# Maxima over the last 260 keys, taken off VectorE in layers 2 and 3 of a four-layer gated cross-attention model

## The chip, the cores and the metric

The kernel runs on one core of one Trainium2 chip. The metric is the device time of one execution in microseconds (us), the median of several runs. The core has TensorE (PE; its weight loads are shown as PEld), VectorE (DVE), ScalarE (ACT), GpSimd (POOL) and SyncE, which issues DMAs (SP).

## The reference

Four layers, each a cross-attention from 1024 queries to 6404 context keys of width 128, followed by a feed-forward part, both gated and added to x. The change touches the attentions of layers 2 and 3, which have 16 heads of width 8. Cut to what matters:

```python
q = heads(norm(x) @ Wq + bq)           # 1024 x 16 x 8
k = heads(ctx @ Wk + bk)               # 6404 x 16 x 8
v = heads(ctx @ Wv + bv)
w = softmax(q @ k.T / sqrt(8))         # over 6404 keys; layer 2 masks keys too
x = x + tanh(g) * ((w @ v) @ Wo + bo)
```

A softmax in this form subtracts the largest score of each query before the exponential.

## The kernel before

`narrow_attention` computes one such layer. It cuts the work into 32 units, one for each head and half of the queries (512 columns, `CH`), so there are 64 units in the two layers. Each unit needs two passes over the keys.

**Maxima.** TensorE computes scores with 128 queries down the partitions and keys along the row, into two slots of two PSUM banks each (banks 4 to 7). A step is two matmuls of 512 keys (`max_score`, L1692) and one VectorE reduction over the 1024 scores (L1858). The 6404 keys are six pairs of 512 and a rest of 260 (`REM`). For each of four groups of 128 queries there are six wide steps, and two more steps reduce the rest of two groups each (L1861), 26 steps in all. VectorE then reduces the seven partial maxima to a negated maximum (`nm`, L1867) and splits it into two bfloat16 parts (`nmp`, L1868 and L1869).

**Exponentials.** `turn_nm` (L1704) transposes the split maximum on TensorE, and ScalarE copies it into the top rows of Q (L1791), so that the next scores come with the maximum already subtracted. TensorE then computes the scores again with 128 keys down the partitions (`score`, L1680), 51 tiles a unit, the last of four keys. ScalarE takes the exponential of each (L1800). The scores and the transposed maxima share a ring of three PSUM banks, 0 to 2: the taker with number n is written when ScalarE has read number n - 3. After each four tiles the weighted sums of the batch before (`weigh`, L1716) run in four column groups into bank 3, and ScalarE copies that bank out once a unit (L1784).

**Order.** All loops are written out by hand, and each engine takes its work in order. TensorE puts the maximum matmuls of the coming units between the scores of the present one: it is a whole unit and 14 matmuls ahead (`ahead = MM + 2 * LEAD`), and behind score t it issues those from `ahead + MM * u + t * MM // ST` on. A step's first matmul waits until VectorE has reduced the step two before it. The transposition for unit u+1 stands behind tile 42 of unit u (`NM_AT` is 43). In the last unit of each layer no maxima are left, and a filler matmul of the same shape (`keep_warm`, L1722) takes their place; that unit also holds the sums over the denominators and the projections. SyncE loads K and Q for each unit ahead of time. GpSimd does nothing in this phase.

The end of one pass on TensorE, with the function that decides when a bank may be written:

```python
for t in range(ST):
    score(u, t)
    ...
    for m in range(ahead + MM * u + t * MM // ST, ahead + MM * u + (t + 1) * MM // ST):
        if m < MM * UNITS:
            max_score(m)
    if t == NM_AT - 1 and u + 1 < UNITS:
        turn_nm(u + 1)
```

Of the kernel before, what the change touches and what calls it, by code (L numbers as in the profile page):

```python
# [9 lines left out]
ALU = mybir.AluOpType  # L10
ACT = mybir.ActivationFunctionType
AX = mybir.AxisListType

P = 128
# [3 lines left out]
S = 6404  # L18
ST = -(-S // P)
LAST = S - (ST - 1) * P  # L20
CH = 512
HALVES = N // CH
# [35 lines left out]
class Core:  # L58
# [18 lines left out]
    def sb(self, name, shape, dtype, held=None):  # L77
        return (held or self.held).enter_context(self.nc.sbuf_tensor(name, shape, dtype))
# [1234 lines left out]
def narrow_attention(c, name, w, gate, masked, scratch):  # L1313
    nc = c.nc
# [3 lines left out]
    ROWS = TOP + 7 * DH  # L1318
    VW = DH + 1
    UNITS = HEADS * HALVES  # L1320
    UQ = CH // P
    PAIR = 2 * CH
    FULL = S // PAIR
    REM = S - FULL * PAIR
    STEPS = UQ * FULL + UQ // 2
    MM = 2 * STEPS
    LEAD = 7
    NM_AT = 43
    SPREAD_AT, PROJECT_AT = (20, 24), (40, 50)
    BATCH = 4  # L1330
    BATCHES = -(-ST // BATCH)
    MROW = 64
# [3 lines left out]
    with ExitStack() as held:  # L1336
        sb = lambda n, s, d=FP32: c.sb(f"{name}_{n}", s, d, held)
# [2 lines left out]
        K = [sb(f"K{i}", [P, S], BF16) for i in range(2)]  # L1340
        Q = [sb(f"Q{i}", [P, CH], BF16) for i in range(3)]
        V = sb("V", [P, ST, HEADS, VW])
        mx = sb("mx", [P, 2, UQ, FULL + 1])
        nm = sb("nm", [P, 2, UQ])
        nmp = sb("nmp", [P, 2, UQ, 2], BF16)
        acc = sb("acc", [P, 2, CH])
# [242 lines left out]
        def step_no(u, i):  # L1589
            return STEPS * u + i  # L1590

        def ring_no(u, t):
            return 1 + (ST + 1) * u + t + (1 if t >= NM_AT and u + 1 < UNITS else 0)

        def nm_no(u):
            return 0 if u == 0 else 1 + (ST + 1) * (u - 1) + NM_AT

        def step_at(i):
            if i < UQ * FULL:
                return [(i // FULL, (i % FULL) * PAIR + half * CH, CH) for half in range(2)]  # L1600
            return [(2 * (i - UQ * FULL) + half, FULL * PAIR, REM) for half in range(2)]

        def slot(step):
            return 4 + 2 * (step % 2)

        ACC = 3
        with phase(nc, "chain", "scored", "exped", "weighed", "max_scored", "maxed", "nm_ready", "acc_out", "acc_clear",
                   "max_in_0", "max_in_1", "max_in_2", "exp_in_0", "exp_in_1", "exp_in_2", "out_in_0", "out_in_1",
                   "den_out", "normal", "projected", "last_projected", "summed") as (
                block, chain, scored, exped, weighed, max_scored, maxed, nm_ready, acc_out, acc_clear,  # L1610
                max_in_0, max_in_1, max_in_2, exp_in_0, exp_in_1, exp_in_2, out_in_0, out_in_1, den_out, normal,
                projected, last_projected, summed):
            out_in = (out_in_0, out_in_1)
            OUT_MOVES = 2 * BATCH
# [6 lines left out]
            def loads_by(u):  # L1621
                return sum(6 if v % HALVES == 0 else 3 for v in range(u % 3, u + 1, 3))
# [49 lines left out]
            def _(pe):  # L1672
# [10 lines left out]
                def max_score(m):  # L1683
# [11 lines left out]
                    if half == 1:  # L1695
                        last.then_inc(max_scored, 1)

                def turn_nm(u):
                    n = nm_no(u)
                    pe.wait_ge(nm_ready, u + 1)  # L1700
                    if n >= 3:
                        pe.wait_ge(exped, n - 2)
                    for j in range(UQ):
                        last = nc.tensor.matmul(c.banks(n % 3)[0:2, j * P:(j + 1) * P], nmp[:, u % 2, j, :], c.identb[:],  # L1704
                                                start=True, stop=True)
                    last.then_inc(scored, 1)
# [38 lines left out]
                    last.then_inc(last_projected, 1)  # L1745

                ahead = MM + 2 * LEAD
                for m in range(ahead):
                    max_score(m)
                    if m == MM + 7:  # L1750
                        turn_nm(0)
                for u in range(UNITS):
                    if u == UNITS - 1:
                        pe.wait_ge(maxed, STEPS * UNITS)
                    for t in range(ST):
                        score(u, t)
                        if u == UNITS - 1:
                            keep_warm(u)
                        for m in range(ahead + MM * u + t * MM // ST, ahead + MM * u + (t + 1) * MM // ST):
                            if m < MM * UNITS:  # L1760
                                max_score(m)
                        if t == NM_AT - 1 and u + 1 < UNITS:
# [15 lines left out]
            @block.scalar  # L1778
            def _(act):
                def take_acc(u):  # L1780
                    act.wait_ge(weighed, BATCHES * (u + 1))
                    if u >= 2:
                        act.wait_ge(out_in[u % 2], 16 * OUT_MOVES * (u // 2))
                    nc.scalar.copy(acc[:, u % 2, :], c.banks(ACC)).then_inc(acc_out, 1)  # L1784

                def take_nm(u):
                    n = nm_no(u)
                    act.wait_ge(scored, n + 1)
                    if u >= 3:
                        act.wait_ge(scored, ring_no(u - 3, ST - 1) + 1)  # L1790
                    nc.scalar.copy(Q[u % 3][0:2, :], c.banks(n % 3)[0:2, :]).then_inc(exped, 1)  # L1791

                take_nm(0)
                for u in range(UNITS):
                    for t in range(ST):
                        n, r, batch = ring_no(u, t), rows_of(t), BATCHES * u + t // BATCH
                        act.wait_ge(scored, n + 1)
                        if t % BATCH == 0 and batch >= 2:
                            act.wait_ge(weighed, batch - 1)
                        nc.scalar.activation(prob[0:r, batch % 2, t % BATCH, :], c.banks(n % 3)[0:r, :], ACT.Exp,  # L1800
                                             scale=SCALE).then_inc(exped, 1)
                        if t == NM_AT - 1 and u + 1 < UNITS:
# [3 lines left out]
                take_acc(UNITS - 1)  # L1806

            @block.vector
            def _(dve):
# [42 lines left out]
                for u in range(UNITS):  # L1852
                    for i in range(STEPS):
                        step = step_no(u, i)
                        j, a, k = step_at(i)[0]
                        dve.wait_ge(max_scored, step + 1)
                        if i < UQ * FULL:
                            nc.vector.tensor_reduce(mx[:, u % 2, j, i % FULL:i % FULL + 1], c.banks(slot(step), 2),  # L1858
                                                    AX.X, ALU.max).then_inc(maxed, 1)
                        else:  # L1860
                            nc.vector.tensor_reduce(mx[:, u % 2, j:j + 2, FULL],  # L1861
                                                    c.ps[:, slot(step):slot(step) + 2, 0:REM],
                                                    AX.X, ALU.max).then_inc(maxed, 1)
                    dve.wait_ge(maxed, step_no(u, STEPS - 1) + 1)
                    if u >= 2:
                        dve.wait_ge(scored, nm_no(u - 2) + 1)
                    link(nc.vector.tensor_reduce(nm[:, u % 2, :], mx[:, u % 2, :, :], AX.X, ALU.max, negate=True))  # L1867
                    link(nc.vector.tensor_copy(nmp[:, u % 2, :, 0], nm[:, u % 2, :]))  # L1868
                    nc.vector.tensor_tensor(nmp[:, u % 2, :, 1], nm[:, u % 2, :], nmp[:, u % 2, :, 0], ALU.subtract  # L1869
                                            ).then_inc(nm_ready, 1)  # L1870
                for f in range(HALVES):
                    add_groups(f)
# [533 lines left out]
```

## Time and profile before

| | |
|---|---|
| median of 3 runs | 5270.39 us (5267.61 to 5272.48) |
| span of the profiled execution, the time given of it | 5269.8 us |
| PE busy | 4827.1 us, 92% |
| DVE busy | 4327.4 us, 82% |
| ACT busy | 3096.7 us, 59% |
| POOL busy | 1940.9 us, 37% |
| one unit in layers 2 and 3 | 31.62 us |

Busy shares are of the whole span; layers 2 and 3 take about the last 40% of it and have no GpSimd work in their main phase. A group of instructions is listed with its line, engine, operation, output and input; then its busy time and the mean duration of one in ns, then the idle time of the engine just before it and what ended that. Durations of matmuls overlap, so that a pitch is read from starts.

### The profile page before, as it was taken

What the parts mean: (1) busy time and instruction counts of PE and PEld (TensorE: products, weight loads), DVE (VectorE), ACT (ScalarE), POOL (GpSimd) and SP (SyncE); (2) the same over time, 40 slices, a digit from 0 to 9 for tenths busy, and PEclk for the clock granted to TensorE, in tenths of its full rate; (3) what the DMA queues carried; (4) which work ended last, traced back from release to release, by engine and by line L of the source; (5) the groups of instructions that cost most, each with busy time, mean ns of one, the idle gap of its engine ahead of it and who ended that gap; (6) DMA issues with size and microseconds to landing.
All of it is one profiled execution on the core that took longest, in us unless ns stands there. A gap on an engine that the chain in (4) does not pass through costs nothing. (4 is left out here: it accounts for less than half of the span.)

```text
span 5269.8 us, 74714 instructions
## 1 busy us (share of the span) xinstructions
PE 4827.1 (92%) x26357; PEld 1891.5 (36%) x26366; DVE 4327.4 (82%) x4358; ACT 3096.7 (59%) x6111; POOL 1940.9 (37%) x1522
## 2 busy tenths in 40 slices
PE   8938999999999999999995699999998699999997
PEld 5623454544545454544442222222222322222222
DVE  7648878788787878878886699999996599999996
ACT  3313454454545454444442288888886288888886
POOL 0014878787787878787783100000000100000000
PEclk9968999999999999999997699999998699999998
DMA  1024334242333334142210211111110211111110
GB/s 36 5 89 117 95 92 112 60 124 51 103 81 98 98 82 122 40 123 64 51 38 15 78 29 29 29 34 29 29 23 2 78 28 29 28 29 33 30 23 6
DMA packets 171375, 298.10 MB, mean 57 GB/s; under 512 B 39061, under 2 KB 108577, under 8 KB 167393
## 3 DMA queue, kind: packets, MB, share of 16 engines
q1 hardware_dynamic: 169420, 292.95, 21.8%
q8 instruction: 213, 3.49, 0.3%
q14 instruction: 158, 1.29, 0.1%
q10 hardware_dynamic: 1584, 0.37, 0.0%
HBM read 187.39 MB, written 101.25 MB: 55 GB/s over the span
## 5 line engine op out<-in xcount | busy, mean ns | idle before, releaser
L1858 DVE TENSOR_REDUCE a_mx<-ps 128x1 f32<-128x1024 f32 x1536 | 1814.5, 1220 | 71.0 <-PE ps L1692 54.5
L1800 ACT ACTIVATE a_prob<-ps 128x512 f32<-128x512 f32 (+1 forms) x3264 | 1699.7, 601 | 288.1 <-PE ps L1680 283.3
L1227 POOL TENSOR_TENSOR tot_p<-tot_p,prob 128x512 f32<-128x512 f32 (+1 forms) x922 | 1300.4, 1410 | 401.5 <-ACT prob L1103 315.3
L1103 ACT ACTIVATE prob<-ps 128x512 f32<-128x512 f32 (+1 forms) x1512 | 801.1, 608 | 866.1 <-PE ps L979 865.2
L1151 DVE TENSOR_REDUCE mx<-ps 128x1 f32<-128x1024 f32 x896 | 1047.3, 1214 | 222.4 <-PE ps L956 222.4
L1692 PE MATMUL ps<-a_K,a_Q 59*128 59x512 bf16 (+1 forms) x3328 | 1094.7, 386 | 56.4 <-DMA a_Q<-q_stack_dram 44.5
L1680 PE MATMUL ps<-a_Q,a_K 59*128 59x512 bf16 (+1 forms) x3264 | 988.7, 383 | 55.8 <-ACT a_prob L1800 49.5
L1716 PE MATMUL ps<-a_prob,a_V 128*9 128x512 f32 x6528 | 871.8, 596 | 10.9 <-ACT a_acc L1784 10.9
L978 PE MATMUL ps<-QA,KA 128*128 128x512 f32 (+1 forms) x1888 | 841.7, 446 | 0.0
L990 PE MATMUL ps<-prob,V 128*64 128x512 f32 x3024 | 801.1, 599 | 0.7 <-ACT prob L1103 0.7
L979 PE MATMUL ps<-QB,KB 128*128 128x512 f32 (+1 forms) x1888 | 746.1, 395 | 0.0
L1173 DVE TENSOR_TENSOR tot_d<-tot_d,prob 128x512 f32<-128x512 f32 x539 | 629.3, 1167 | 134.6 <-ACT prob L1103 114.8
L1680 PEld LDWEIGHTS ps<-a_Q,a_K 59*128 59x128 bf16 (+1 forms) x3264 | 240.6, 93 | 1114.5 <-ACT a_prob L1800 920.3
L978 PEld LDWEIGHTS ps<-QA,KA 128*128 128x128 f32 (+1 forms) x1888 | 351.4, 186 | 279.0 <-ACT prob L1103 109.7
L2299 POOL MEMSET f_ones<- 128x128 f32 x1 | 0.2, 210 | 1097.5 <-POOLq L43 1097.5
L2208 POOL MEMSET f_spread<- 8x512 f32 x1 | 0.5, 515 | 1095.4 <-SPq L41 1095.4
L956 PE MATMUL ps<-KM,QM 64*128 64x512 bf16 (+1 forms) x1920 | 319.1, 383 | 69.2 <-DVE mx L1151 42.6
L979 PEld LDWEIGHTS ps<-QB,KB 128*128 128x128 f32 (+1 forms) x1888 | 354.0, 187 | 61.8 <-issue 26.8
L1692 PEld LDWEIGHTS ps<-a_K,a_Q 59*128 59x128 bf16 x3328 | 240.3, 94 | 357.5 <-DVE a_mx L1858 301.8
L990 PEld LDWEIGHTS ps<-prob,V 128*64 128x64 f32 x3024 | 224.3, 136 | 392.5 <-issue 323.6
L1227 POOL TENSOR_TENSOR tot_p<-tot_p,h 128x512 f32<-128x512 f32 x230 | 323.6, 1407 | 99.8 <-ACT h L1103 78.0
L1103 ACT ACTIVATE h<-ps 128x512 f32<-128x512 f32 (+1 forms) x376 | 212.5, 607 | 220.4 <-PE ps L979 220.3
(415 smaller groups left out, 3772.8 us busy)
## 6 DMA issues: line engine op xcount, KB each, us to landing
a_K<-k_stack_dram SPq DMA_DIRECT2D x128, 300.2 KB
k_hi_dram<-hi_s SPq DMA_DIRECT2D x112, 256.0 KB, 2.2
k_lo_dram<-lo_s SPq DMA_DIRECT2D x112, 256.0 KB, 2.4
KA<-k_hi_dram SPq DMA_DIRECT2D x64, 384.0 KB, 4.3
KA<-k_lo_dram SPq DMA_DIRECT2D x64, 384.0 KB, 5.6
KB<-k_hi_dram SPq DMA_DIRECT2D x64, 384.0 KB, 6.6
k_bf_dram<-bf_s SPq DMA_DIRECT2D x112, 128.0 KB, 1.8
KM<-k_bf_dram SPq DMA_DIRECT2D x32, 448.0 KB
```

The lines of the kernel that those rows point to most:

```text
L978: nc.tensor.matmul(out, KA[:, cols], QA[u % 2][:], start=True, stop=False)
L979: nc.tensor.matmul(out, KB[:, cols], QB[u % 2][:], start=False, stop=True).then_inc(scored, 1)
L990: last = nc.tensor.matmul(c.banks(ACC)[DH * g:DH * (g + 1), :], V[:, t, DH * side:DH * (side + 1)], prob_of(u, t), start=(t < 2), stop=(t ...
L1103: nc.scalar.activation(prob_of(u, t)[0:r, :], c.banks(n % 3)[0:r, :], ACT.Exp, scale=SCALE).then_inc(exped, 1)
L1151: nc.vector.tensor_reduce(mx[:, u % 2, j, i % FULL:i % FULL + 1], c.banks(slot(n), 2), AX.X, ALU.max).then_inc(released, 1)
L1173: nc.vector.tensor_tensor(tot_d[0:r, u % 2, :], tot_d[0:r, u % 2, :], p, ALU.add).then_inc(totalled_d, 1)
L1227: nc.gpsimd.tensor_tensor(tot_p[0:r, u % 2, :], tot_p[0:r, u % 2, :], p, ALU.add).then_inc(totalled_p, 1)
L1680: nc.tensor.matmul(c.banks(n % 3)[0:r, :], K[(u // HALVES) % 2][0:ROWS, t * P:t * P + r], Q[u % 3][0:ROWS, :], start=True, stop=True).then ...
L1692: last = nc.tensor.matmul(c.banks(slot(step) + half)[:, 0:k], Q[u % 3][MROW:MROW + ROWS, j * P:(j + 1) * P], K[(u // HALVES) % 2][MROW:MRO ...
L1716: last = nc.tensor.matmul(c.banks(ACC)[32 * g:32 * g + VW, :], V[:, t, u // HALVES, :], prob[:, (BATCHES * u + b) % 2, g, :], start=(t < B ...
L1800: nc.scalar.activation(prob[0:r, batch % 2, t % BATCH, :], c.banks(n % 3)[0:r, :], ACT.Exp, scale=SCALE).then_inc(exped, 1)
L1858: nc.vector.tensor_reduce(mx[:, u % 2, j, i % FULL:i % FULL + 1], c.banks(slot(step), 2), AX.X, ALU.max).then_inc(maxed, 1)
```

## The change

The steps over the last 260 keys leave the maxima's slots and VectorE. Four times in a unit (behind tiles 6, 13, 20 and 27, and at the start for unit 0) TensorE computes 260 scores of one group of 128 queries into a bank of the exponentials' ring, and ScalarE copies them to SBUF (`tail`). GpSimd folds them in five rounds, each time taking the maximum of the two halves as max(a - b, 0) + b, from 260 to 130, 65, 33, 17 and 9 columns for each of four groups; the nine go into `mx` beside the six others. VectorE waits for the fold before it takes the negated maximum, over 15 values instead of 7. The split into two bfloat16 parts moves to GpSimd, and the transposition waits for that.

```diff
-    STEPS = UQ * FULL + UQ // 2
+    STEPS = UQ * FULL
+    TAIL_AT = (6, 13, 20, 27)
+    LEFT = 9
...
+                def score_tail(u, j):
+                    n = tail_no(u, j)
+                    if j == 0:
+                        pe.wait_ge(max_in[u % 3], 16 * loads_by(u))
+                    if n >= 3:
+                        pe.wait_ge(exped, n - 2)
+                    nc.tensor.matmul(c.banks(n % 3)[:, 0:REM], Q[u % 3][MROW:MROW + ROWS, j * P:(j + 1) * P],
+                                     K[(u // HALVES) % 2][MROW:MROW + ROWS, FULL * PAIR:S], start=True, stop=True
+                                     ).then_inc(scored, 1)
...
                 def turn_nm(u):
                     n = nm_no(u)
-                    pe.wait_ge(nm_ready, u + 1)
+                    pe.wait_ge(nm_cut, 2 * (u + 1))
...
+                        if t in TAIL_AT and u + 1 < UNITS:
+                            score_tail(u + 1, TAIL_AT.index(t))
...
+                def take_tail(u, j):
+                    n = tail_no(u, j)
+                    act.wait_ge(scored, n + 1)
+                    if j == 0 and u >= 1:
+                        act.wait_ge(folded, u)
+                    nc.scalar.copy(tail[:, j, :], c.banks(n % 3)[:, 0:REM]).then_inc(exped, 1)
...
+                def fold_tail(u):
+                    pool.wait_ge(exped, tail_no(u, UQ - 1) + 1)
+                    if u >= 2:
+                        pool.wait_ge(nm_ready, u - 1)
+                    src, w = tail, REM
+                    for dst in (half, fold, half, fold, None):
+                        n = -(-w // 2)
+                        to = mx[:, u % 2, :, FULL:FULL + LEFT] if dst is None else dst[:, :, 0:n]
+                        a, b, d = src[:, :, 0:n], src[:, :, w - n:w], over[:, :, 0:n]
+                        link(nc.gpsimd.tensor_tensor(d, a, b, ALU.subtract))
+                        link(nc.gpsimd.tensor_scalar(d, d, 0.0, None, ALU.max))
+                        last = nc.gpsimd.tensor_tensor(to, d, b, ALU.add)
+                        if dst is None:
+                            last.then_inc(folded, 1)
+                        else:
+                            link(last)
+                        src, w = dst, n
+
+                def cut_nm(u):
+                    pool.wait_ge(nm_ready, u + 1)
+                    if u >= 2:
+                        pool.wait_ge(scored, nm_no(u - 2) + 1)
+                    nc.gpsimd.tensor_copy(nmp[:, u % 2, :, 0], nm[:, u % 2, :]).then_inc(nm_cut, 1)
+                    pool.wait_ge(nm_cut, 2 * u + 1)
+                    nc.gpsimd.tensor_tensor(nmp[:, u % 2, :, 1], nm[:, u % 2, :], nmp[:, u % 2, :, 0], ALU.subtract
+                                            ).then_inc(nm_cut, 1)
...
-                        else:
-                            nc.vector.tensor_reduce(mx[:, u % 2, j:j + 2, FULL],
-                                                    c.ps[:, slot(step):slot(step) + 2, 0:REM],
-                                                    AX.X, ALU.max).then_inc(maxed, 1)
...
                     dve.wait_ge(maxed, step_no(u, STEPS - 1) + 1)
+                    dve.wait_ge(folded, u + 1)
                     if u >= 2:
-                        dve.wait_ge(scored, nm_no(u - 2) + 1)
-                    link(nc.vector.tensor_reduce(nm[:, u % 2, :], mx[:, u % 2, :, :], AX.X, ALU.max, negate=True))
-                    link(nc.vector.tensor_copy(nmp[:, u % 2, :, 0], nm[:, u % 2, :]))
-                    nc.vector.tensor_tensor(nmp[:, u % 2, :, 1], nm[:, u % 2, :], nmp[:, u % 2, :, 0], ALU.subtract
+                        dve.wait_ge(nm_cut, 2 * (u - 1))
+                    nc.vector.tensor_reduce(nm[:, u % 2, :], mx[:, u % 2, :, :], AX.X, ALU.max, negate=True
                                             ).then_inc(nm_ready, 1)
```

## Rows read from the trace of the kernel before

**Rows 1.** The page's first line.

```profile
span 5269.8 us, 74714 instructions
```

**Rows 2.** Groups by line; busy us, mean ns, idle before it and its releasers.

```profile
L1858 DVE TENSOR_REDUCE a_mx<-ps 128x1 f32<-128x1024 f32 x1536 | 1814.5, 1220 | 71.0 <-PE ps L1692 54.5
```

**Rows 3.** VectorE's timeline in a steady unit; start, length, instructions merged.

```profile
3300.07 3.76 DVE L1858 TENSOR_REDUCE a_mx<-ps 128x1 f32<-128x1024 f32 x3
...
3331.69 3.71 DVE L1858 TENSOR_REDUCE a_mx<-ps 128x1 f32<-128x1024 f32 x3
```

**Rows 4.** VectorE's timeline at the start of the phase in layer 2.

```profile
2985.35 28.22 DVE L1858 TENSOR_REDUCE a_mx<-ps 128x1 f32<-128x1024 f32 x24 [9.03 <-PE ps L1692]
...
3015.51 4.70 DVE L1858 TENSOR_REDUCE a_mx<-ps 128x1 f32<-128x1024 f32 x4
```

**Rows 5.** TensorE's timeline over one batch of four tiles in that unit.

```profile
3315.54 0.39 PE L1680 MATMUL ps<-a_Q,a_K 59*128 59x512 bf16 x1
...
3316.62 0.39 PE L1680 MATMUL ps<-a_Q,a_K 59*128 59x512 bf16 x1
...
3316.94 1.05 PE L1716 MATMUL ps<-a_prob,a_V 128*9 128x512 f32 x8
3317.92 0.39 PE L1680 MATMUL ps<-a_Q,a_K 59*128 59x512 bf16 x1
```

**Rows 6.** ScalarE's timeline around and in the last unit of layer 3.

```profile
5193.51 1.54 ACT L1800 ACTIVATE a_prob<-ps 128x512 f32<-128x512 f32 x3 [0.31 <-PE ps L1680]
5195.32 2.06 ACT L1800 ACTIVATE a_prob<-ps 128x512 f32<-128x512 f32 x4 [0.27 <-PE ps L1680]
...
5202.68 2.06 ACT L1800 ACTIVATE a_prob<-ps 128x512 f32<-128x512 f32 x4 [0.31 <-PE ps L1680]
5205.05 2.06 ACT L1800 ACTIVATE a_prob<-ps 128x512 f32<-128x512 f32 x4 [0.31 <-PE ps L1680]
```

**Rows 7.** ScalarE's timeline in the steady unit: its end, and the maximum's batch.

```profile
3306.24 1.54 ACT L1800 ACTIVATE a_prob<-ps 128x512 f32<-128x512 f32 x3 [0.31 <-PE ps L1680]
3308.60 2.07 ACT L1800 ACTIVATE a_prob<-ps 128x512 f32<-128x512 f32 x4 [0.81 <-PE ps L1680]
...
3332.58 1.57 ACT L1800 ACTIVATE a_prob<-ps 128x512 f32<-128x512 f32 x3 [0.31 <-PE ps L1680]
...
3335.44 2.07 ACT L1800 ACTIVATE a_prob<-ps 128x512 f32<-128x512 f32 x4 [0.36 <-PE ps L1680]
```

**Rows 8.** Groups by line and shape, GpSimd's and one of ScalarE's.

```profile
L1227 POOL TENSOR_TENSOR tot_p<-tot_p,prob 128x512 f32<-128x512 f32 x897 | 1268.9, 1415 | 357.5 <-ACT prob L1103 271.5 <-ACT h L1103 0.4
L1245 POOL TENSOR_TENSOR y<-y,fin_s 128x512 f32<-128x512 f32 x32 | 50.9, 1591 | 2.5
L1232 POOL TENSOR_TENSOR tot_p<-tot_p,tot_d 128x512 f32<-128x512 f32 x32 | 40.6, 1268 | 4.6
L1224 POOL COPY tot_p<-prob 128x512 f32<-128x512 f32 x26 | 15.8, 609 | 55.4 <-ACT prob L1103 55.4
L1530 POOL TENSOR_SCALAR a_keepm<-a_keepv 128x51 f32<-128x51 f32 x1 | 0.3, 255 | 0.2 <-POOL a_keepv L1529 0.2
L1529 POOL COPY a_keepv<-keep 4x1 f32<-4x1 f32 x1 | 0.2, 178 | 0.1
...
L1054 ACT CAST hi_s<-ps 128x260 fp32r<-128x260 f32 x8 | 3.1, 393 | 0.0
```

**Rows 9.** Stretches of 1 us in the last unit; busy us (instructions) of each engine, granted clock, DMA.

```profile
5210.00:5211.00 1.00, 0.50 (x6) 0.10 (x2) 0.95 (x2) 0.84 (x2) 0.00 (x0) 1.00 0.00 0
...
5214.00:5215.00 1.00, 1.00 (x8) 0.00 (x0) 0.97 (x2) 0.56 (x2) 0.00 (x0) 0.50 0.00 0
...
5217.00:5218.00 1.00, 1.00 (x10) 0.11 (x4) 0.97 (x2) 0.85 (x2) 0.00 (x0) 1.00 0.00 0
```

**Rows 10.** TensorE's timeline there.

```profile
5213.32 1.90 PE L1716 MATMUL ps<-a_prob,a_V 128*9 128x512 f32 x8
...
5216.88 1.04 PE L1716 MATMUL ps<-a_prob,a_V 128*9 128x512 f32 x8
```

More of the change, by code:

```diff
@@ L1342, in narrow_attention @@
         V = sb("V", [P, ST, HEADS, VW])
-        mx = sb("mx", [P, 2, UQ, FULL + 1])
+        mx = sb("mx", [P, 2, UQ, FULL + LEFT])
+        tail = sb("tail", [P, UQ, REM])
+        half, fold, over = sb("half", [P, UQ, REM // 2]), sb("fold", [P, UQ, REM // 4]), sb("over", [P, UQ, REM // 2])
         nm = sb("nm", [P, 2, UQ])
@@ L1590, in step_no, with takes_ring, tail_no @@
             return STEPS * u + i
+        ring = {}
+        def takes_ring(kind, u, i):
+            ring[kind, u, i] = len(ring)
+        for j in range(UQ):
+            takes_ring("tail", 0, j)
+        takes_ring("nm", 0, 0)
+        for u in range(UNITS):
+            for t in range(ST):
+                takes_ring("score", u, t)
+                if t in TAIL_AT and u + 1 < UNITS:
+                    takes_ring("tail", u + 1, TAIL_AT.index(t))
+                if t == NM_AT - 1 and u + 1 < UNITS:
+                    takes_ring("nm", u + 1, 0)
         def ring_no(u, t):
-            return 1 + (ST + 1) * u + t + (1 if t >= NM_AT and u + 1 < UNITS else 0)
+            return ring["score", u, t]
         def nm_no(u):
-            return 0 if u == 0 else 1 + (ST + 1) * (u - 1) + NM_AT
+            return ring["nm", u, 0]
+        def tail_no(u, j):
+            return ring["tail", u, j]
         def step_at(i):
-            if i < UQ * FULL:
-                return [(i // FULL, (i % FULL) * PAIR + half * CH, CH) for half in range(2)]
-            return [(2 * (i - UQ * FULL) + half, FULL * PAIR, REM) for half in range(2)]
+            return [(i // FULL, (i % FULL) * PAIR + half * CH, CH) for half in range(2)]
         def slot(step):
@@ L1607, in narrow_attention @@
         with phase(nc, "chain", "scored", "exped", "weighed", "max_scored", "maxed", "nm_ready", "acc_out", "acc_clear",
+                   "folding", "folded", "nm_cut",
                    "max_in_0", "max_in_1", "max_in_2", "exp_in_0", "exp_in_1", "exp_in_2", "out_in_0", "out_in_1",
@@ L1610, in narrow_attention @@
                 block, chain, scored, exped, weighed, max_scored, maxed, nm_ready, acc_out, acc_clear,
-                max_in_0, max_in_1, max_in_2, exp_in_0, exp_in_1, exp_in_2, out_in_0, out_in_1, den_out, normal,
+                folding, folded, nm_cut, max_in_0, max_in_1, max_in_2, exp_in_0, exp_in_1, exp_in_2, out_in_0, out_in_1, den_out, normal,
                 projected, last_projected, summed):
@@ L1747, in _ @@
                 ahead = MM + 2 * LEAD
+                for j in range(UQ):
+                    score_tail(0, j)
                 for m in range(ahead):
@@ L1761, in _ @@
                                 max_score(m)
+                        if t in TAIL_AT and u + 1 < UNITS:
+                            score_tail(u + 1, TAIL_AT.index(t))
                         if t == NM_AT - 1 and u + 1 < UNITS:
@@ L1791, in take_nm @@
                     nc.scalar.copy(Q[u % 3][0:2, :], c.banks(n % 3)[0:2, :]).then_inc(exped, 1)
+                def take_tail(u, j):
[4 more added lines that the diff above has]
+                    nc.scalar.copy(tail[:, j, :], c.banks(n % 3)[:, 0:REM]).then_inc(exped, 1)
+                for j in range(UQ):
+                    take_tail(0, j)
                 take_nm(0)
@@ L1801, in _ @@
                                              scale=SCALE).then_inc(exped, 1)
+                        if t in TAIL_AT and u + 1 < UNITS:
+                            take_tail(u + 1, TAIL_AT.index(t))
                         if t == NM_AT - 1 and u + 1 < UNITS:
@@ L1806, in _ @@
                 take_acc(UNITS - 1)
+            @block.gpsimd
+            def _(pool):
+                link = Chain(pool, folding)
+                def fold_tail(u):
[23 more added lines that the diff above has]
+                                            ).then_inc(nm_cut, 1)
+                fold_tail(0)
+                cut_nm(0)
+                for u in range(1, UNITS):
+                    fold_tail(u)
+                    cut_nm(u)
             @block.vector
@@ L1856, in _ @@
                         dve.wait_ge(max_scored, step + 1)
-                        if i < UQ * FULL:
-                            nc.vector.tensor_reduce(mx[:, u % 2, j, i % FULL:i % FULL + 1], c.banks(slot(step), 2),
-                                                    AX.X, ALU.max).then_inc(maxed, 1)
-                        else:
-                            nc.vector.tensor_reduce(mx[:, u % 2, j:j + 2, FULL],
-                                                    c.ps[:, slot(step):slot(step) + 2, 0:REM],
-                                                    AX.X, ALU.max).then_inc(maxed, 1)
+                        nc.vector.tensor_reduce(mx[:, u % 2, j, i % FULL:i % FULL + 1], c.banks(slot(step), 2),
+                                                AX.X, ALU.max).then_inc(maxed, 1)
                     dve.wait_ge(maxed, step_no(u, STEPS - 1) + 1)
+                    dve.wait_ge(folded, u + 1)
                     if u >= 2:
-                        dve.wait_ge(scored, nm_no(u - 2) + 1)
-                    link(nc.vector.tensor_reduce(nm[:, u % 2, :], mx[:, u % 2, :, :], AX.X, ALU.max, negate=True))
-                    link(nc.vector.tensor_copy(nmp[:, u % 2, :, 0], nm[:, u % 2, :]))
-                    nc.vector.tensor_tensor(nmp[:, u % 2, :, 1], nm[:, u % 2, :], nmp[:, u % 2, :, 0], ALU.subtract
+                        dve.wait_ge(nm_cut, 2 * (u - 1))
+                    nc.vector.tensor_reduce(nm[:, u % 2, :], mx[:, u % 2, :, :], AX.X, ALU.max, negate=True
                                             ).then_inc(nm_ready, 1)
```

## The prediction

> **What bounds the kernel now.** I read the page first, then the groups by line, then the timelines of one steady unit on VectorE, ScalarE and TensorE, then the same timeline in the last unit, where one of the engines has nothing to do. The span is 5269.8 us [rows 1], and nothing else is given of this execution's time; the median of the runs is 5270.39 us, 0.6 more, so I add differences to 5270. By the groups the maxima look like the bound: L1858 is the costliest group and VectorE sits idle before it for only 71 us in 1536 times [rows 2]. A steady unit of layers 2 and 3 takes 31.62 us (3300.07 to 3331.69, both the first maximum after a negated maximum) [rows 3]; there are 64 of them.
>
> But VectorE alone would be faster. At the start of the phase, with no exponentials, a whole unit of its work, 24 wide maxima, two narrow ones and three small operations, runs from 2985.35 to 3015.51, 30.16 us, 1.174 us for a wide maximum ((28.22 - 1.22) / 23) [rows 4]. What really sets the pace shows in one batch of four key tiles [rows 5]. First score at 3315.54, fourth score at 3316.62, when the first exponential has given back its bank of the ring of three; the weighted sums at 3316.94; the next first score at 3317.92. That is 2.38 us for a batch, and two wide maxima need 2.35. Is it VectorE that holds this loop? In the last unit no maxima are left, only fillers of the same shape, and the batch still takes 2.37 us (5202.68 to 5205.05) [rows 6]. So the loop is TensorE and ScalarE handing over three banks, and VectorE merely just keeps up. VectorE shows as the bound at one place: the three-tile batch at a unit's end takes 2.36 us (3306.24 to 3308.60) [rows 7], and 1.81 us (5193.51 to 5195.32) where there are no maxima to wait for [rows 6]. Without VectorE a unit is 31.62 - 0.55 = 31.07 us.
>
> **What is removed.** Two narrow maxima and two small operations leave VectorE, about 30.16 - 24 x 1.174 = 1.98 us less 0.2 for the remaining reduction, 1.8 us a unit. Because of the loop that is worth only the 0.55 us at the end of each unit; after the change just one maximum matmul falls there instead of two, and VectorE has slack. The last two units of each layer have no such wait, so 60 x 0.55 = -33 us. At each start 26 steps become 24, which is 1.5 us, against four copies ahead of everything and GpSimd's split: I take -1 us for both layers. The first fold lies under the first 28 us of maxima and costs nothing.
>
> **What is added to the ring.** Four times a unit (behind tiles 6, 13, 20, 27) a 260-column matmul takes a bank and ScalarE copies it. A ScalarE read of 128x260 took 393 ns [rows 8]; an exponential takes 0.60 us by itself and its pitch in a row of four is (2.06 - 0.60) / 3 = 0.49 us [rows 6], 0.52 with the handover of a bank. The loop is tight, so it matters which bank the last score of the batch waits for. Behind tiles 6 and 13 there is one more full exponential ahead of the weighted sums: +0.52 each. Behind tile 20 the fifth taker waits for the short copy: +0.30. Behind tile 27 the copy's own matmul is last and short: +0.41. Sum 1.75 us. The trace has this case already: the batch in which the negated maximum takes a bank is 2.86 us (3332.58 to 3335.44) [rows 7], +0.49. Bounds: 4 x 0.30 = 1.2 and 4 x 0.52 = 2.1 us. ScalarE itself has room. 62 units carry copies: 62 x 1.75 = +108 us.
>
> **What is added on GpSimd, and who waits.** The fold has five rounds with 520, 260, 132, 68 and 36 elements a partition, 1016 in all, each a subtraction, a maximum with zero and an addition, each waiting for the one before. No such fold is in the trace. A tensor_tensor of 512 took 1268 ns, and the smallest copy 178 ns [rows 8]: with 178 ns fixed the slope is 2.13 ns an element, and ten of them cost 10 x 0.178 + 2 x 1016 x 0.00213 = 6.1 us. The tensor_scalar of 51 took 255 ns [rows 8], so (255 - 178) / 51 = 1.5 ns an element: 5 x 0.178 + 1.016 x 1.5 = 2.4 us. Fourteen handovers at 2.5 / 32 = 0.08 us (idle ahead of L1245) [rows 8] are 1.1 us. F = 9.6 us. Lower bound: a fixed part of 0.1, single-source rounds at the copy's price (609 for 512) and half the gaps, 8.0 us. Upper bound: the 1415 ns form for the two-source ones, that price for the maxima too, and double gaps, 12 us.
>
> The Trainium skill, "GPSIMD Engine Reference", section 3.1, gives about 2.6 cycles an element for a two-source operation at 1.2 GHz, and its section 4 sends elementwise work to VectorE instead; by it the ten would cost an estimated 4.4 us and their dispatch. The 1268 ns row agrees.
>
> Now place it. The fold starts when the fourth copy is done, about 0.15 us after score 28 is issued. TensorE then goes on at 2.37 us a batch and issues score 41 at 3 x 2.37 + 0.22 = 7.33 us. TensorE is 14 maximum matmuls ahead: behind score 36 it has issued the last of unit u+1, and behind 37 to 40 the first four of unit u+2, which fill both slots. The one behind score 41 waits until VectorE has reduced the first of them. VectorE takes things in order, and stands at its new wait for the fold ahead of the negated maximum. So TensorE is released at R = 0.15 + F + 0.3 (reduction of 0.2 and handover) + 1.25 (one wide maximum) = F + 1.7 = 11.3 us. Behind TensorE's wait stand the scores, the weighted sums and the transposition of the maximum, so ScalarE runs dry too. Undisturbed, score 44 would be issued at 7.11 + 2.87 = 9.98; now at R + 2.1 (two scores, the transposition, the weighted sums; the bank wait of 0.5 is hidden). The stall costs F + 3.8 - 9.98 = F - 6.2 = 3.4 us a unit; 1.8 with the lower bound, 5.8 with the upper. In the two units 30 TensorE only waits at the transposition itself, F - 7.2 = 2.4. Sum 60 x 3.4 + 2 x 2.4 = +209 us. The split on GpSimd is two operations of about 0.2 us and ends before VectorE's first wide maximum: nothing. VectorE's wait for the split of two units ago was met a unit earlier, as was ScalarE's for the fold before: nothing.
>
> **The clock.** TensorE stands idle from about 7.6 to 11.3, 3.7 us in every unit. In the last unit it did little in 5210 to 5212 (busy 0.50 in the first of these), with the granted clock at 1.00; then it was granted 0.50 (1.2 of 2.4 GHz) at 5214, and 1.00 again at 5217 [rows 9]. In that spell one batch, weighted sums at 5213.32 to those at 5216.88, took 3.56 us [rows 10]: 1.2 more than 2.37. Nothing in a steady unit idles as long now. I expect the clock to fall in each stall: 62 x 1.2 = +74 us, with zero and 2.4 us a unit as bounds (back before work resumes; two such batches).
>
> The Trainium skill, "TensorE: Matmul & The Clock Gate", in its table of advice, asks for no long idle gaps between bursts of matmuls, or the rate is halved; the trace agrees, having the fall after even shorter ones. If the stall were short enough not to break that advice, the sum would be the warm case below.
>
> **Sum.** 108 + 209 - 33 - 1 = +283 warm, +357 with the clock falling: 5270 + 357 = 5627 us.
>
> **Rivals.** (a) The stall is there, but the clock holds: 5270 + 283 = 5553. For it: work resumes soon, and the fall in the last unit came after a mixture of waits. (b) No stall: the fold takes under 6.2 us, that is 0.6 of my sum. Then only the ring's cost is left, 108 - 34: 5344. Against it: the ten two-source operations alone are 6.1. (c) Faster: VectorE is the bound after all, and each hole in the loop is one that VectorE's lateness made. Then a unit falls to 24 x 1.174 + 0.2 and today's two small waits of 0.3, 29.0 us, and 62 x 2.6 = -161: 5109. It decides only if the copies stay within VectorE's 28.4 us and the fold under 6.2 us. For it: the 71 us idle in 1536. Against: the 2.37 us batch without maxima. (d) The two cancel, 5270: it needs the fold under 6.2 and copies at half their price. The change surely does what it says: the narrow maxima go, the copies and folds come.
>
> **Chances.** Clock falls 0.52 (5627), warm stall 0.28 (5553), no stall 0.10 (5344), faster 0.06, no change 0.02, beyond (double spells, fold of over 12 us) 0.02. A measurement tells 0.2%, 10 us, from no change. Faster 0.06, same 0.02, slower 0.92. With the lower fold and no clock fall the time is 5553 - 60 x 1.6 = 5457; with the upper fold and one spell 5627 + 60 x 2.4 = 5771, of which I take the nearer part, since the upper bound piles three dear prices up. Range 5455 to 5720.
>
> **What the profile after would show.** L1858's successor still at 1.18 us, but VectorE idle before the reduction into a_nm, put down to GpSimd, 2 us or more, 62 times. Fold rounds of 1.3, about 1 and 1.3 us, falling; from first to last 9.6 us. ScalarE's batches with a copy 2.7 to 2.9 us apart, others 2.37, and the three-tile batch 1.8. A unit of about 37 us; TensorE idle 3.7 us in each, and the granted clock 0.5 behind it. If no GpSimd wait stands before a_nm, step F is wrong; if batches with a copy take 2.37, the ring step is; if clock rows read 1.00 throughout, the clock step is.

## The result and the profile after

| | before | after |
|---|---|---|
| median | 5271.43 us (4 runs beside the changed kernel) | 5853.34 us (5849.41 to 5855.75) |
| ratio | | 1.1104 (1.1088 to 1.112) |
| span of the profiled execution | 5269.8 us | 5854.0 us |
| one unit in layers 2 and 3 | 31.62 us | 40.96 us |

Slower, as forecast, but by 582 us where 357 were forecast, and outside the range of 5455 to 5720.

The page of the changed kernel: the span and, in 40 slices, the granted clock of TensorE in tenths.

```profile
span 5854.0 us, 76061 instructions
...
PEclk9969999999999999999679999999976899999998
```

The clock's digits hide what happens in layers 2 and 3: 9 means 90% or more, and a fall to half the clock for 6 to 7 us in 41 leaves some 0.92 (0.91 is measured over 3300 to 3500).

The groups of the changed kernel (busy us, mean ns, idle before, releaser). The first answers to [rows 2].

```profile
L1941 DVE TENSOR_REDUCE a_mx<-ps 128x1 f32<-128x1024 f32 x1536 | 1819.9, 1220 | 523.9 <-PE ps L1714 522.5
L1845 ACT ACTIVATE a_prob<-ps 128x512 f32<-128x512 f32 (+1 forms) x3264 | 1733.0, 605 | 760.4 <-PE ps L1702 760.3
```

A wide maximum costs what it did, and VectorE's idle time ahead of one went from 71 us to 524, ScalarE's ahead of an exponential from 288 to 760. Both wait for TensorE. Whom does TensorE wait for? VectorE's timeline from one negated maximum to the next, answering to [rows 3]:

```profile
3504.05 0.22 DVE L1947 TENSOR_REDUCE a_nm<-a_mx 128x4 f32<-128x60 f32 x1 [4.19 <-POOL a_mx L1870]
3504.18 3.56 DVE L1941 TENSOR_REDUCE a_mx<-ps 128x1 f32<-128x1024 f32 x3
3509.97 2.35 DVE L1941 TENSOR_REDUCE a_mx<-ps 128x1 f32<-128x1024 f32 x2 [2.23 <-PE ps L1714]
...
3539.59 1.23 DVE L1941 TENSOR_REDUCE a_mx<-ps 128x1 f32<-128x1024 f32 x1 [0.93 <-PE ps L1714]
3545.01 0.21 DVE L1947 TENSOR_REDUCE a_nm<-a_mx 128x4 f32<-128x60 f32 x1 [4.20 <-POOL a_mx L1870]
```

The unit is 40.96 us (3504.05 to 3545.01). VectorE waits 4.2 us for GpSimd's fold, as it does 62 times (259.9 us). GpSimd's groups by shape, answering to [rows 8], the five shapes of the maximum with zero (L1869) and the two largest and two smallest of the others:

```profile
L1869 POOL TENSOR_SCALAR a_over<-a_over 128x520 f32<-128x520 f32 x64 | 96.2, 1504 | 5.6
L1870 POOL TENSOR_TENSOR a_half<-a_over,a_tail 128x520 f32<-128x520 f32 x64 | 76.5, 1195 | 5.3
L1868 POOL TENSOR_TENSOR a_over<-a_tail 128x520 f32<-128x520 f32 x64 | 70.8, 1106 | 1876.1 <-ACT a_tail L1834 1876.1
L1869 POOL TENSOR_SCALAR a_over<-a_over 128x260 f32<-128x260 f32 x64 | 55.0, 859 | 5.6
...
L1869 POOL TENSOR_SCALAR a_over<-a_over 128x132 f32<-128x132 f32 x64 | 34.5, 539 | 5.6
...
L1869 POOL TENSOR_SCALAR a_over<-a_over 128x68 f32<-128x68 f32 x64 | 24.2, 378 | 5.6
...
L1869 POOL TENSOR_SCALAR a_over<-a_over 128x36 f32<-128x36 f32 x64 | 19.1, 298 | 5.6
L1868 POOL TENSOR_TENSOR a_over<-a_fold 128x36 f32<-128x36 f32 x64 | 16.9, 265 | 5.0
L1870 POOL TENSOR_TENSOR a_mx<-a_over,a_fold 128x36 f32<-128x36 f32 x64 | 16.6, 259 | 5.3
```

A fold lasts from 3534.46 to 3544.92, 10.46 us. TensorE's timeline through the stall of that unit, answering to [rows 5, 10]:

```profile
3534.38 0.39 PE L1702 MATMUL ps<-a_Q,a_K 59*128 59x512 bf16 x1
...
3540.20 0.39 PE L1702 MATMUL ps<-a_Q,a_K 59*128 59x512 bf16 x1 [0.25 <-ACT a_prob L1845]
3540.87 0.39 PE L1714 MATMUL ps<-a_K,a_Q 59*128 59x512 bf16 x1 [0.28 <-DVE a_mx L1941]
3541.19 1.04 PE L1748 MATMUL ps<-a_prob,a_V 128*9 128x512 f32 x8
3542.16 0.39 PE L1702 MATMUL ps<-a_Q,a_K 59*128 59x512 bf16 x1
...
3542.39 0.38 PE L1702 MATMUL ps<-a_Q,a_K 59*128 59x512 bf16 x1
3546.41 0.60 PE L1714 MATMUL ps<-a_K,a_Q 59*128 59x512 bf16 x1 [3.65 <-DVE a_mx L1941]
...
3548.43 1.90 PE L1748 MATMUL ps<-a_prob,a_V 128*9 128x512 f32 x8
3550.26 0.60 PE L1702 MATMUL ps<-a_Q,a_K 59*128 59x512 bf16 x1
```

Score 28 is issued at 3534.38, score 41 at 3542.39, and the maximum matmul behind it, the fifth of the unit after next, at 3546.41, when VectorE has reduced the first one. That is the stall at the place that was forecast, and the durations behind it (0.60 and 1.90 instead of 0.39 and 1.05) are those of the lower clock. The clock itself, in stretches of 1 us (PE busy first; the eighth number, after five engines, is the granted clock), answering to [rows 9]:

```profile
3544.00:3545.00 1.00, 0.00 (x0) 0.00 (x0) 0.00 (x0) 0.00 (x0) 0.74 (x3) 1.00 0.43 77
3545.00:3546.00 1.00, 0.00 (x0) 0.00 (x0) 0.99 (x2) 0.00 (x0) 0.39 (x2) 0.86 0.16 24
3546.00:3547.00 1.00, 0.59 (x3) 0.13 (x3) 1.00 (x2) 0.00 (x0) 0.00 (x0) 0.50 0.05 8
...
3552.00:3553.00 1.00, 0.94 (x6) 0.22 (x9) 1.00 (x2) 0.96 (x2) 0.00 (x0) 0.73 0.00 0
```

TensorE is granted 1.2 GHz, half of its 2.4, from late in its idle time until some 6 us after work resumes.

ScalarE's timeline gives every batch, from the start of its row to the next; answering to [rows 7]:

```profile
3520.97 2.07 ACT L1845 ACTIVATE a_prob<-ps 128x512 f32<-128x512 f32 x4 [0.51 <-PE ps L1702]
3524.00 1.08 ACT L1845 ACTIVATE a_prob<-ps 128x512 f32<-128x512 f32 x2 [0.97 <-PE ps L1702]
...
3529.41 0.60 ACT L1845 ACTIVATE a_prob<-ps 128x512 f32<-128x512 f32 x1 [0.31 <-PE ps L1702]
...
3532.05 2.06 ACT L1845 ACTIVATE a_prob<-ps 128x512 f32<-128x512 f32 x4 [0.29 <-PE ps L1702]
3533.98 0.41 ACT L1834 COPY a_tail<-ps 128x260 f32<-128x260 f32 x1
3534.81 2.06 ACT L1845 ACTIVATE a_prob<-ps 128x512 f32<-128x512 f32 x4 [0.42 <-PE ps L1702]
```

Batch by batch: those that start with tiles 20 and 24, with a copy each, take 2.64 and 2.76 us, as forecast. But the one of tiles 8 to 11 (3520.97 to 3524.00), with no copy, takes 3.03, and so does 36 to 39 just before the stall. Nothing in the prediction makes those long.

**A theory for them.** The change makes 48 maximum matmuls of 52 and leaves the rule `t * MM // ST` alone. With 52 in 51 tiles, a step's first half stood behind an even tile and its second behind the odd one that follows, throughout (two stand behind tile 50). With 48, none stands behind tiles 0, 17 and 34, and from tile 1 to 16 and from 35 on the halves straddle: each step's first half stands behind an odd tile and its second behind the even one after it, which makes second, first, second, first in a batch. The second half comes right after the weighted sums, VectorE, which ran dry during these, needs 1.2 us for it, and the first half at the end of the batch waits for that reduction: 3540.87 above. The fourth tile's matmul and the weighted sums stand behind it. I call it the theory of the straddling halves; its rival was that the ring or ScalarE's copies lengthen these batches.

### The profile page after: what moved, and what is told of

It is laid out like the page before. It is cut to its first block and busy times, and to the rows that moved or that the text cites. A ratio compares the mean times of both kernels' runs of the same rounds, so it can differ in the third digit from the quotient of the medians.

```text
span 5854.0 us, 76061 instructions
## 1 busy us (share of the span) xinstructions
PE 4995.3 (85%) x26366; PEld 1904.9 (33%) x26366; DVE 4235.2 (72%) x4102; ACT 3186.0 (54%) x6367; POOL 2557.7 (44%) x2610
## 5 line engine op out<-in xcount | busy, mean ns | idle before, releaser
L1845 ACT ACTIVATE a_prob<-ps 128x512 f32<-128x512 f32 (+1 forms) x3264 | 1733.0, 605 | 760.4 <-PE ps L1702 760.3
L1714 PE MATMUL ps<-a_K,a_Q 59*128 59x512 bf16 x3072 | 1098.1, 424 | 266.8 <-DVE a_mx L1941 260.7
L1702 PE MATMUL ps<-a_Q,a_K 59*128 59x512 bf16 (+1 forms) x3264 | 1085.5, 411 | 195.4 <-ACT a_prob L1845 189.3
L1748 PE MATMUL ps<-a_prob,a_V 128*9 128x512 f32 x6528 | 931.3, 634 | 0.3 <-ACT a_acc L1820 0.3
L1868 POOL TENSOR_TENSOR a_over<-a_tail 128x520 f32<-128x520 f32 x64 | 70.8, 1106 | 1876.1 <-ACT a_tail L1834 1876.1
L990 PE MATMUL ps<-h,V 128*64 128x512 f32 x752 | 282.8, 599 | 0.0
```

What stands on the lines that cost most here:

```text
L990: last = nc.tensor.matmul(c.banks(ACC)[DH * g:DH * (g + 1), :], V[:, t, DH * side:DH * (side + 1)], prob_of(u, t), start=(t < 2), stop=(t ...
L1702: nc.tensor.matmul(c.banks(n % 3)[0:r, :], K[(u // HALVES) % 2][0:ROWS, t * P:t * P + r], Q[u % 3][0:ROWS, :], start=True, stop=True).then ...
L1714: last = nc.tensor.matmul(c.banks(slot(step) + half)[:, 0:k], Q[u % 3][MROW:MROW + ROWS, j * P:(j + 1) * P], K[(u // HALVES) % 2][MROW:MRO ...
L1748: last = nc.tensor.matmul(c.banks(ACC)[32 * g:32 * g + VW, :], V[:, t, u // HALVES, :], prob[:, (BATCHES * u + b) % 2, g, :], start=(t < B ...
```

## The experiments

### The halves in step again

```diff
+        def beside(t):
+            return min(max(t - 2, 0), MM)
...
-                        for m in range(ahead + MM * u + t * MM // ST, ahead + MM * u + (t + 1) * MM // ST):
+                        for m in range(ahead + MM * u + beside(t), ahead + MM * u + beside(t + 1)):
```

> The changed kernel, with the maximum matmuls placed between the scores so that a step's two halves always stand behind an even and the following odd tile (none behind tiles 0, 1 and 50); in the change none stands behind 0, 17 and 34, so that from 1 to 16 and from 35 on the halves straddle. Theory of the halves: where they straddle, the third matmul of a batch waits for a reduction that could start only after the weighted sums, 0.66 us a batch (3.03 instead of 2.37); batches without a copy then all take 2.37 us. The batch before the stall gains too, but the stall takes that back, so 1.1 to 1.8 us a unit, 5745 to 5785 us, nearest 5765. Rival, the ring's copies or ScalarE make those batches long: they stay at 3.03 and the time at 5853 within 10.

Measured 5783.02 us (5781.02 to 5784.44), ratio to before 1.0966 (1.0944 to 1.0987). ScalarE's timeline:

```profile
3504.13 2.06 ACT L1848 ACTIVATE a_prob<-ps 128x512 f32<-128x512 f32 x4 [0.52 <-PE ps L1705]
3506.50 1.08 ACT L1848 ACTIVATE a_prob<-ps 128x512 f32<-128x512 f32 x2 [0.31 <-PE ps L1705]
```

The batch of tiles 8 to 11 takes 2.37 us instead of 3.03, and the time is within the range of the theory and 70 us from the rival's. The stall still takes much of the gain back. It also changes a little: the fifth maximum matmul of the unit after next now stands behind score 40, one tile earlier. TensorE's timeline, from score 40 to score 44:

```profile
3523.83 0.39 PE L1705 MATMUL ps<-a_Q,a_K 59*128 59x512 bf16 x1
3528.73 0.61 PE L1717 MATMUL ps<-a_K,a_Q 59*128 59x512 bf16 x1 [4.52 <-DVE a_mx L1944]
...
3533.28 0.60 PE L1705 MATMUL ps<-a_Q,a_K 59*128 59x512 bf16 x1
```

TensorE stands idle for 4.52 us instead of 3.65, and score 44 comes 4.55 us after the release instead of 3.85.

### The copies earlier, so that the fold is in time

```diff
-    TAIL_AT = (6, 13, 20, 27)
+    TAIL_AT = (2, 5, 8, 11)
```

> The changed kernel with the four copies behind tiles 2, 5, 8 and 11 instead of 6, 13, 20 and 27, so that the fold ends some ten tiles before VectorE wants it. Theory of the late fold: VectorE's idle time ahead of the negated maximum goes from 4.2 us to nothing, TensorE's clock stays at 1.00, and the unit falls from 40.96 to 35.4 to 36.0 us: 5500 to 5545 us, nearest 5528. Rival, GpSimd's work itself or the ring is what costs: the time falls by less than 150 us.

Measured 5507.37 us (5505.28 to 5507.79), ratio 1.0442 (1.0422 to 1.0463). No idle time stands before the negated maximum, the clock is 1.00 over 3300 to 3500, and 346 us are gone. The long batches stay. ScalarE's timeline of this run shows a batch of 2.38 us and then the one of tiles 36 to 39, 3.03 us:

```profile
3505.30 2.06 ACT L1845 ACTIVATE a_prob<-ps 128x512 f32<-128x512 f32 x4 [0.31 <-PE ps L1702]
3507.68 2.07 ACT L1845 ACTIVATE a_prob<-ps 128x512 f32<-128x512 f32 x4 [0.31 <-PE ps L1702]
3510.71 1.57 ACT L1845 ACTIVATE a_prob<-ps 128x512 f32<-128x512 f32 x3 [0.97 <-PE ps L1702]
```

### Both

> Both of these together: only the four bank takers are left of the cost. Theory of the ring: unit 31.07 + 1.75 = 32.8 us, 5344 us, between 5310 (four at 0.30) and 5370 (four at 0.52). Rival, VectorE was the bound before: then two narrow maxima less give 5271 or below, down to 5109.

Measured 5350.59 us (5348.49 to 5352.84), ratio 1.0146 (1.0126 to 1.0166). VectorE's timeline, from one negated maximum to the next:

```profile
3507.27 0.22 DVE L1950 TENSOR_REDUCE a_nm<-a_mx 128x4 f32<-128x60 f32 x1
...
3540.18 0.22 DVE L1950 TENSOR_REDUCE a_nm<-a_mx 128x4 f32<-128x60 f32 x1
```

A unit is 32.91 us, where 32.8 was forecast for the four bank takers alone. VectorE has lost its two narrow maxima and all that was left on it hides, GpSimd's fold is in time, and the kernel is still 78 us slower than before. So it is not VectorE that sets the pace. Together with the run before, the straddling halves cost 157 us where there is no stall to absorb them.

### TensorE kept busy through the stall

```diff
+                def fill(u):
+                    n = ring_no(u, 42)
+                    pe.wait_ge(exped, n - 2)
+                    for _ in range(8):
+                        nc.tensor.matmul(c.banks(n % 3)[:, 0:432], c.ident[:],
+                                         V[:, 0:3, :, :].rearrange("p t g v -> p (t g v)"), start=True, stop=True)
...
+                        if t == 41 and u + 2 < UNITS:
+                            fill(u)
```

> The changed kernel with eight filler matmuls of 432 float32 columns on TensorE behind score 41 in units 0 to 29, into the bank that score 42 overwrites, where TensorE otherwise stands idle for 3.8 us. They should last 3.0 to 3.4 us, less than the wait. Theory of the clock: the granted clock stays at 1.00, score 44 comes 2.1 us after TensorE is released instead of 3.8, so 1.7 to 1.9 us less a unit, 60 units, 5740 to 5750 us. Rival, the clock row is no cause and the slow restart is the ring's: 5853 or, if the fillers outlast the wait, above.

Measured 5873.31 us (5870.48 to 5874.05), ratio 1.1136 (1.1114 to 1.1158): a miss. I had the fillers' length wrong. TensorE's timeline:

```profile
3504.43 6.07 PE L1761 MATMUL ps<-a_V,ident 128*128 128x432 f32 x16
3510.43 0.39 PE L1714 MATMUL ps<-a_K,a_Q 59*128 59x512 bf16 x1
...
3512.58 0.39 PE L1702 MATMUL ps<-a_Q,a_K 59*128 59x512 bf16 x1
```

Eight float32 fillers are sixteen passes of 0.38 us, 6.07 in all, 2.4 us more than the 3.65 of the wait. What follows is at full clock: score 44 comes 2.15 us after the release (my R + 2.1), where the changed kernel took 3.85. The same with half of them:

> The run with fillers again, but four instead of eight: eight lasted 6.07 us against a wait of 3.8, while the clock stayed at 1.00 and score 44 came 2.15 us after TensorE was released instead of 3.85. Four last 3.04 us and fit inside the wait. Theory of the clock: 1.7 to 2.0 us less in each of 60 units, 5733 to 5751 us. Rival, what eight fillers gave back was given by something other than the clock: 5853.

Measured 5747.0 us (5746.38 to 5748.35), ratio 1.0898 (1.0881 to 1.0915). Useless work in the stall makes the kernel 106 us faster, 1.8 us a unit, although TensorE still waits for VectorE; the granted clock is 1.00 over 3300 to 3500:

```profile
3520.15 3.17 PE L1761 MATMUL ps<-a_V,ident 128*128 128x432 f32 x8
3523.88 0.39 PE L1714 MATMUL ps<-a_K,a_Q 59*128 59x512 bf16 x1 [0.56 <-DVE a_mx L1950]
```

A further run was planned, the changed kernel with a single two-source maximum on GpSimd in place of the three operations of each round. It gave no result, so what a shorter fold does in the late places is not measured.

### The most that VectorE's relief could give

The kernel before with these lines, and with the first experiment's `beside`:

```diff
-    STEPS = UQ * FULL + UQ // 2
+    STEPS = UQ * FULL
...
-                        if i < UQ * FULL:
-                            nc.vector.tensor_reduce(mx[:, u % 2, j, i % FULL:i % FULL + 1], c.banks(slot(step), 2),
-                                                    AX.X, ALU.max).then_inc(maxed, 1)
-                        else:
-                            nc.vector.tensor_reduce(mx[:, u % 2, j:j + 2, FULL],
-                                                    c.ps[:, slot(step):slot(step) + 2, 0:REM],
-                                                    AX.X, ALU.max).then_inc(maxed, 1)
```

> The kernel before without the maxima over the last 260 keys at all (the maximum is taken over the first 6144 keys; nothing goes through the ring, GpSimd does nothing), halves behind even and odd tiles as in the first run. It is the most that taking them off VectorE could give. Theory of the loop between TensorE and ScalarE: a unit of 31.07 us, 5272 - 33 - 3 = 5236 us, 5230 to 5242. Rival, VectorE was the bound: 24 wide maxima and three small operations, 29.1 us a unit, 5115 us.

Measured 5252.24 us (5251.8 to 5253.15), ratio 0.996 (0.9946 to 0.9973). Two narrow maxima a unit for nothing, with nothing put in their place, are worth 21 us of the 5273. That is far from the 5115 of a bound VectorE and also short of 5236. ScalarE's timeline says where the rest is:

```profile
3483.61 1.58 ACT L1803 ACTIVATE a_prob<-ps 128x512 f32<-128x512 f32 x3 [0.30 <-PE ps L1683]
...
3486.76 2.07 ACT L1803 ACTIVATE a_prob<-ps 128x512 f32<-128x512 f32 x4 [0.55 <-PE ps L1683]
3489.13 1.54 ACT L1803 ACTIVATE a_prob<-ps 128x512 f32<-128x512 f32 x3 [0.31 <-PE ps L1683]
3490.95 2.07 ACT L1803 ACTIVATE a_prob<-ps 128x512 f32<-128x512 f32 x4 [0.28 <-PE ps L1683]
```

The last batch of the unit has its 1.82 us, but the batch of the negated maximum takes 3.15 instead of 2.86: with this placing VectorE comes to it from its three small operations, a little late. The run with both edits has the same placing and only one small operation there, and its batch took 2.87 us (3509.37 to 3512.24). A unit of the run here is 31.32 us.

### Two attempts at a better kernel

The kernel before, the doubled maximum matmuls moved from tile 50 to the longer batch of the negated maximum:

```diff
+        def beside(t):
+            return t if t <= 42 else 44 if t == 43 else min(t + 2, MM)
```

> The kernel before, with all its work, but the extra two maximum matmuls of a unit stand behind tiles 42 and 43, where the batch is longer, and not behind tile 50. Theory: VectorE needs 30.16 us a unit, the loop 31.07, and only the wait at the unit's end, 0.55 us, was VectorE's; of it 0.2 to 0.5 us come back, 5240 to 5260 us. Rival, VectorE's lateness only moves to the next batches, 5272 within 5, or the pairs straddling cost more, above 5280.

Measured 5277.18 us (5273.0 to 5348.92, ten of the eleven below 5281), ratio 1.0019 (0.9993 to 1.0044). The end of the unit fell to 1.82 us and the batch of the negated maximum rose to 3.47: the wait moved. Then the part of the change that costs the ring nothing, alone, `cut_nm` on GpSimd with `pe.wait_ge(nm_cut, 2 * (u + 1))` in `turn_nm`, as in the diff of the change:

> The kernel before with one part of the change alone: the split of the negated maximum into two bfloat16 parts on GpSimd; all narrow maxima stay on VectorE. It frees VectorE of 0.4 us a unit and lengthens the way to the transposition by some 0.5 us, which stands four tiles later. Theory of the loop: VectorE already stands idle for 1.1 us a unit before the batch in which it is awaited, so nothing comes of it, 5272 within 6. Rival, VectorE's total is the bound: 62 x 0.4 = 25 us less, 5248.

Measured 5272.28 us (5269.57 to 5275.32), ratio 0.9998 (0.9989 to 1.0007): no difference. And both:

> The same, and the extra two maximum matmuls of a unit behind tiles 42 and 43 instead of behind 50. Alone that moved VectorE's lateness: the unit's last batch fell from 2.36 to 1.82 us, that of the negated maximum rose from 2.86 to 3.47. There VectorE comes from three small operations; with two of them gone it is 0.4 us earlier. Theory: that batch takes 3.1 to 3.2 us, 0.25 to 0.35 less a unit than before, 5250 to 5258 us. Rival, three wide maxima in one batch are too many whatever stands ahead of them: 5272 within 6.

Measured 5277.91 us (5276.02 to 5279.7), ratio 1.0009 (1.0 to 1.0018). A miss: the batch still takes 3.47 us, so the two small operations ahead were not what made it long, and the length fits three wide maxima in one batch (3.5 us at 1.174). ScalarE's timeline of this run:

```profile
3492.80 1.58 ACT L1803 ACTIVATE a_prob<-ps 128x512 f32<-128x512 f32 x3 [0.31 <-PE ps L1683]
...
3496.27 2.06 ACT L1803 ACTIVATE a_prob<-ps 128x512 f32<-128x512 f32 x4 [0.97 <-PE ps L1683]
```

No version beats the kernel before by more than the 21 us that leaving the work out gives.

## Where the prediction was right and where it failed

Two steps failed: "VectorE has slack", by which the straddling halves had no term, and the sizes of the stall and of the clock's fall. The bound, the ring's price and the place of the stall were right. By the runs the 581 us split into these parts (differences of medians, the late fold taken away first):

| part | forecast, us | shown, us | by |
|---|---|---|---|
| bank takers, less the wait at the unit's end, and the start | 108 - 33 - 1 = 74 | 78 | both edits, against before |
| straddling halves, without a stall | none | 157 | early copies, with and without them |
| stall without the clock | 209 | 240 | early copies (346) less the clock's part |
| the clock | 74 | 106 | four fillers |
| sum | 357 | 581 | |

**The order matters.** The parts overlap. If the halves are put in step first, with the late fold still in place, they are worth 70 us (5853 to 5783), and stall and clock together cost 432 (5783 less 5351), not 346; 283 were forecast. So the halves alone don't explain the miss: with them repaired the time is 5783, still above the range. Part of what the lower clock costs lay under the straddling waits. The batch from score 44 to score 48 takes 3.39 us in the changed kernel and 3.04 with four fillers, 0.35 for the clock; with the halves in step it takes 3.17 at the lower clock, where 2.37 is the full-clock loop, 0.80.

**The bound.** Right, and shown twice: without the narrow maxima the time falls by 21 us at most, and with them hidden and only the bank takers added it rises by 78. The 33 us for the unit's end were 21 in the run without the narrow maxima: the last batch lost its 0.54 us, and the batch of the negated maximum gained 0.29. VectorE's 71 us of idle time looked like a bound because its 2.35 us for two wide maxima and the loop's 2.37 are nearly equal.

**The ring's price.** Right in its sum: 1.75 us a unit forecast, and 1.84 by the measured 32.91 and the derived 31.07. That run has its copies in other places, two of them in one batch. In the places of the change, with the halves in step (the first experiment), the four cost 0.73, 0.49, 0.27 and 0.38 us, 1.87 in all; 0.52, 0.52, 0.30 and 0.41 were forecast. The first was too cheap in the forecast, perhaps since its batch also holds ScalarE's copy of the accumulator, which I did not test: the two batches of tiles 4 to 11 take 5.73 us (3500.77 to 3506.50) where they took 5.00 before (3310.97 to 3315.97).

**The removed work.** The step "after the change just one maximum matmul falls there instead of two, and VectorE has slack" failed. I looked only at tile 50. I had even worked out from the same rule at which tile each maximum matmul stands behind 36 to 41, and did not ask which half it was. The slack is there on average (24 x 1.174 us in a unit of 31), but not where a batch needs it: with two slots, VectorE can't work ahead. The three-tile batch at the unit's end, for which 1.8 us was forecast, takes 2.14 in the changed kernel (3513.11 to 3515.25) and 1.82 with the halves in step (3536.87 to 3538.69). In the order of the table this is 157 us of the 224 that are missing, in the other order 70.

**The fold.** F was 10.46 us, forecast 9.6 with 8 to 12 as bounds. The ten two-source operations took 5.7 us (6.1 forecast) and the gaps 1.2 (1.1). The five maxima with zero took 1.504 + 0.859 + 0.539 + 0.378 + 0.298 = 3.6 us where I had 2.4: the mis-sized term. I had its slope from one row of 51 elements; the range took the two-source price as the dear end, and by its price the five are 3.4.

**The stall.** In the place forecast. R counted from score 28 was 3546.41 - 3534.38 = 12.03 us; the rule F + 1.7 gives 12.16. The part shown is 31 us above the forecast; the longer fold alone would be 60 x 0.86 = 52 us above, and the batch that the halves delay before the stall (0.67 us, score 41 later) works against it, some 40 us. These two would give 221; the other 19 stay open, and I did not take them apart by a run.

**The clock.** The fall was forecast, and it is a cause: useless matmuls in the wait give 1.8 us a unit back. The term of 1.2 us, one batch, was too small: the lower clock lasts some 6 us of work, over the batches of tiles 40 and 44. With four fillers score 44 comes 2.42 us after the release instead of 3.85, and the batch behind it is 0.35 shorter, 1.78 in all; 2.4 was the upper bound. The Trainium skill, "TensorE: Matmul & The Clock Gate", in its table of advice, warns of idle gaps between bursts; the runs agree, 3.65 us of idle time lowered the clock and 0.56 behind fillers did not.

**The rivals.** (a), the warm stall, is refuted by the 0.50 in the clock's rows; (b), no stall, became the run with both edits, 5351 us against 5344 forecast; (c), VectorE as the bound, is refuted by the run without the narrow maxima, 5252 and not 5109.

## What to carry to other kernels

When an engine looks like the bound (VectorE had 30.16 us of work in a unit of 31.62), look for a stretch in which it has no work but the loop runs on. If the loop keeps its period there, relieving the engine buys little (21 us here), and work put into the loop's own ring costs its full handover. When a count changes in a rule that interleaves two streams (`t * MM // ST`), write out which half of which step falls behind which tile; with double buffering an engine with slack on average can still be late in every batch. A wait of an in-order engine on a long serial chain should be placed by the chain's length, and here a wait of 3.65 us on TensorE was paid a second time in clock, 1.8 us each. Parts that overlap give different prices in different orders, so remove them in both.

## What was unexpected of the hardware

GpSimd's maximum with a constant over 520 elements took 1504 ns, more than its subtraction (1106 ns) or addition (1195 ns) of two tensors of that size. Between 36 and 520 elements the slopes are (1504 - 298) / 484 = 2.5, 1.7 and 1.9 ns an element. The Trainium skill, "GPSIMD Engine Reference", section 4, sets GpSimd against VectorE and calls its one-input operations roughly line-rate and its two-input ones some two times slower; here, on GpSimd itself, the one-input maximum is the dearer of the two, and the measurement decides. No run has these operations on VectorE. A float32 matmul of 432 columns against a full 128x128 tile took two passes of 0.38 us each (eight of them are sixteen records and 6.07 us), so 0.76 us.
